# Keys of 42 chunks turned through device memory instead of on TensorE

## What is computed

```python
q = jax.nn.relu(q) + EPS                      # q, k, v = layernorm(x) @ Wq, Wk, Wv
k = jax.nn.relu(k) + EPS
k_cumsum = jnp.cumsum(k, axis=2)
context = jnp.cumsum(jnp.einsum('bhnd,bhne->bhnde', k, v), axis=2)
D_inv = 1.0 / jnp.einsum('bhnd,bhnd->bhn', k_cumsum, q)
attn = jnp.einsum('bhnd,bhnde,bhn->bhne', q, context, D_inv)
x = x + attn @ Wo + bo
...
gate, y = fp4_linear(x, w_gate), fp4_linear(x, w_up)
x = x + fp4_linear(jax.nn.silu(gate) * y, w_down)
```

## Time and profile before

| | |
|---|---|
| median of 3 runs | 1554.55 us (1552.29 to 1557.08) |
| the profiled execution | 1555.95 us, of which the span from first to last instruction is 1553.7 us |
| granted TensorE clock | 0.997 of full speed |
| PE busy | 1500.2 us, 97% |
| PEld, DVE, ACT, POOL busy | 90%, 73%, 41%, 47% |
| DMA packets on SP's queue | 159120, 129.75 MB, 28.2% of 16 engines' time |

### The profile page before, as it was taken

The page is one execution under the profiler, slowest core; times in us unless marked ns, Lnnn a source line. Parts: engine busy times, 40 slices in busy tenths (PEclk is TensorE's granted clock), DMA queues, the critical chain, the costliest instruction groups (busy, mean ns, idle before and its releaser), DMA issues.

```text
span 1553.7 us, 55070 instructions
## 1 busy us (share of the span) xinstructions
PE 1500.2 (97%) x23652; PEld 1400.9 (90%) x23652; DVE 1131.7 (73%) x2322; ACT 644.2 (41%) x1165; POOL 727.4 (47%) x822
## 2 busy tenths in 40 slices
PE   8989999999999999999999999999999999999998
PEld 7888899889989999999889989899999999989998
DVE  8787676867777777676767777767767777767767
ACT  6433344344443344444344443444443343442433
POOL 4322454443554444554443555444554544554543
PEclk9999999999999999999999999999999999999999
DMA  4102233233233223233233233233233232232210
GB/s 165 33 2 58 71 97 110 79 88 98 82 97 107 87 83 101 79 97 110 75 93 93 86 98 101 78 98 93 77 107 93 80 103 84 83 110 85 75 58 16
DMA packets 159360, 133.25 MB, mean 86 GB/s; under 512 B 12944, under 2 KB 150672, under 8 KB 159120
## 3 DMA queue, kind: packets, MB, share of 16 engines
q1 hardware_dynamic: 159120, 129.75, 28.2%
HBM read 68.09 MB, written 61.60 MB: 83 GB/s over the span
## 4 chain that ended last, share of the span: by engine, by line
issue 23%; PE 18%; DVE 17%; POOL 15%; DMA 13%; SPq 7%; ACT 3%; DVEq 0%; POOLq 0%; ACTq 0%
PE bank L591 12%; DMA attn<-attn_away 4%; DMA hq_away<-hq_blocks 4%; DMA attn_away<-probs 4%; POOL attnT_lo L1499 4%; DVE attn L1861 3%; DVE hq_blocks L1930 3%; SPq L530 3%; POOL hqT_lo L1511 3%; POOL x_bias L1460 2%; POOL xq L1538 2%; POOL hq L1487 2%; SPq L547 2%; ACT attnT_hi L1185 1%; PE bank L795 1%
## 5 line engine op out<-in xcount | busy, mean ns | idle before, releaser
L591 PE MATMUL bank<-xT_hi,wqk_hi 128*128 128x256 f32 x1024 | 211.3, 288 | 1.3 <-DVE hqT_lo L1679 1.3
L591 PE MATMUL bank<-xT_hi,wqk_lo 128*128 128x256 f32 x1024 | 203.7, 280 | 0.0
L591 PE MATMUL bank<-xT_lo,wqk_hi 128*128 128x256 f32 x1024 | 203.6, 280 | 0.0
L1538 POOL TENSOR_TENSOR xq<-x_scaled,x_scale 128x256 f32<-128x256 f32 x64 | 57.9, 904 | 310.6 <-DVE x_scaled L1726 310.6
L1112 ACT ACTIVATE qkT<-bank 128x512 f32<-128x512 f32 x256 | 148.5, 592 | 122.7 <-PE bank L591 120.4
L1499 POOL TENSOR_TENSOR attnT_lo<-attn,attnT_hi 128x1024 fp32r<-128x1024 f32 x58 | 156.9, 2705 | 62.3 <-ACT attnT_hi L1185 62.3
L1559 POOL TENSOR_SCALAR qkT<-qkT 128x512 f32<-128x512 f32 x256 | 158.4, 631 | 34.3 <-ACT qkT L1112 33.2
L591 PEld LDWEIGHTS bank<-xT_hi,wqk_hi 128*128 128x128 f32 x1024 | 157.2, 188 | 5.1 <-issue 1.9
L591 PEld LDWEIGHTS bank<-xT_hi,wqk_lo 128*128 128x128 f32 x1024 | 156.7, 188 | 0.0
L591 PEld LDWEIGHTS bank<-xT_lo,wqk_hi 128*128 128x128 f32 x1024 | 156.6, 188 | 0.0
L1235 ACT ACTIVATE silu<-bank 128x352 f32<-128x352 f32 x128 | 58.4, 457 | 229.2 <-PE bank L591 229.2
(11 more groups left out here) (219 smaller groups left out, 3869.9 us busy)
## 6 DMA issues: line engine op xcount, KB each, us to landing
attn<-attn_away SPq DMA_DIRECT2D x232, 128.0 KB, 2.9
hq_away<-hq_blocks SPq DMA_DIRECT2D x58, 384.0 KB, 3.2
hq<-hq_away SPq DMA_DIRECT2D x232, 96.0 KB, 2.2
attn_away<-probs SPq DMA_DIRECT2D x58, 256.0 KB, 2.7
attn_away<-probs SPq DMA_DIRECT2D x116, 128.0 KB, 2.7
x_in<-in_L_attn_x SPq DMA_DIRECT2D x32, 256.0 KB, 2.9
out<-out_sb SPq DMA_DIRECT2D x64, 128.0 KB, 2.6
qkT<-in_L_attn_Wq SPq DMA_DIRECT2D x1, 1024.0 KB, 7.5
```

The lines of the kernel that those rows point to most:

```text
L591: at = pe.matmul(dst, lhs_at(kt), rhs_at(kt), start=first and kt == 0, stop=last and kt == k_tiles - 1)
L1538: pool.tensor_tensor(blocks(xq[:], XB), blocks(x_scaled[:], XB), each(x_scale[:], XB), ALU.mult).then_inc(xq_ready, 1)
```

## The change

For 42 chunks (`SENT_K`: those from chunk 6 to 61 with c < 3) TensorE's 8 transposes and ACT's 2 copies are gone. Instead DVE transposes the 32x32 blocks of the keys straight from `qkT` into `probs` (`block_k`), SP sends `probs` to one of two buffers in device memory (`k_away`), and eight DMAs fetch it: four for the rows and heads that the early keys read, four for the late ones. The two parts lie in different halves of `k_tok`, so each waits only for the readers of its own half in the chunk before. Both chunks of a unit are blocked by DVE in the odd step ahead of the unit.

In `k_tok` the columns of a head come in the order in which pairs are grouped; `head_keys` finds them. The order in which query and key tiles are projected is changed, so that the four key tiles come first, and `scores` now waits for six tiles of the unit, not four, before its first product. The early keys are ahead of probs by values for every c. SP's order in odd steps is changed: `send_attn` now stands between `send_hq` and `fetch_hq`.

```diff
+    SENT_K = [g for g in range(WARM + 2, END) if g % CHUNKS < CHUNKS - 1]
...
+        k_away = nc.dram_tensor("k_away", (2, P, INNER), F32, kind="Internal").ap()
...
-        QK_ORDER = [0, 4, 2, 6, 1, 5, 3, 7]
+        QK_ORDER = [4, 5, 6, 7, 0, 2, 1, 3]
+        def first_pairs_ready(u):
+            return PAIRS * u + (6 if u else 4)
...
+        k_blocks = probs[:, 0:INNER].rearrange("p (a h c j) -> p h j a c", a=GROUPS, h=2, c=GROUP)
...
+            def send_k(n):
+                sp.wait_ge(k_blocks_ready, sent_k(n) + 1)
+                if sent_k(n) > 1:
+                    sp.wait_ge(early_k_back, 16 * GROUPS * (sent_k(n) - 1))
+                    sp.wait_ge(late_k_back, 16 * GROUPS * (sent_k(n) - 1))
+                sp.dma_start(k_away[sent_k(n) % 2], probs[:, 0:INNER]).then_inc(k_sent, 16)
+            def fetch_k(n, late, back):
+                at = k_away[sent_k(n) % 2].rearrange("(i r) (a h e) -> a h r i e", r=GROUP, a=GROUPS, h=2)
+                to = k_tok[:].rearrange("p (h i e) -> p h i e", h=2, i=GROUPS)
+                for a in range(GROUPS):
+                    h = int((a >= GROUPS // 2) != late)
+                    sp.dma_start(to[GROUP * a:GROUP * (a + 1), h], at[a, h]).then_inc(back, 16)
+            def fetch_early_k(n):                       # fetch_late_k: the same with kv_done
+                sp.wait_ge(k_sent, 16 * (sent_k(n) + 1))
+                sp.wait_ge(kv_early_done, (CHUNKS - 1) * b + c)
+                fetch_k(n, False, early_k_back)
...
                 if c % 2 == 0:                          # SP, after store(g - 4)
+                    if g in SENT_K:
+                        fetch_late_k(g)
+                    if g + 1 in SENT_K:
+                        fetch_early_k(g + 1)
...
                 else:
+                    if g in SENT_K:
+                        fetch_late_k(g)
                     if g - 3 in SENT_HQ:
                         send_hq(g - 3)
+                    if g in SENT_ATTN:
+                        send_attn(g)
+                    if g - 3 in SENT_HQ:
                         fetch_hq(g - 3)
                     if g in SENT_ATTN:
-                        send_attn(g)
                         fetch_attn(g)
+                    if g + 1 in SENT_K:
+                        send_k(g + 1)
+                        fetch_early_k(g + 1)
+                    if g + 2 in SENT_K:
+                        send_k(g + 2)
...
-                pe.wait_ge(qk_ready, PAIRS * u + 4)
+                pe.wait_ge(qk_ready, first_pairs_ready(u))
...
-                if c == 0:
-                    early_keys()
+                early_keys()
...
-                    if c and not first:
-                        early_keys()
...
-                    turn_k(b, c, g)
+                    if g not in SENT_K:
+                        turn_k(b, c, g)
...
+                if n == 0 and g in SENT_K and c % 2 == 0:      # DVE, mask
+                    dve.wait_ge(k_sent, 16 * sent_k(g + 2))
...
+            def block_k(n):
+                t = n % 2
+                dve.wait_ge(qk_ready, PAIRS * (n // 2) + 4)
+                dve.wait_ge(attn_sent, 48 * sent_attn(n - t))
+                if sent_k(n):
+                    dve.wait_ge(k_sent, 16 * sent_k(n))
+                dve.transpose(k_blocks, qkT[:, PAIRS:2 * PAIRS, t * P:(t + 1) * P].rearrange(
+                    "p (h j) (a c) -> p h j a c", h=2, c=GROUP)).then_inc(k_blocks_ready, 1)
...
                 gated_by_silu(g - 2, 0)                        # DVE, odd_step
+                if g + 1 in SENT_K:
+                    block_k(g + 1)
                 if exists(u + 2, ALL_HALVES):
                     ln1_begin(u + 2, c // 2)
...
                 begin_h(g - 2)
+                if g + 2 in SENT_K:
+                    block_k(g + 2)
```

More of the change, by code:

```diff
@@ L1318, in even_step @@
                     square_h(g - 3)
[L1319 to L1320 removed]
+                if g not in SENT_K:
+                    for n in range(2):
+                        keys_to_tokens(b, c, n)
                 high_xq(g - 2)
```

44 lines of the change are left out of this document (32 added, 12 removed).

## The result

The changed kernel takes 1586.51 us in the median of four runs (1582.08 to 1588.4), the kernel before 1553.42 beside it: a ratio of 1.0212 with a 95% interval of 1.0191 to 1.0233. It is slower by 33 us; 1538 was predicted, and the range ended at 1565.

A forecast was written before the change was run, and what follows sets the result against it. PE, busy 1500.2 of 1553.7 us, and its few waits were taken to set the end. Gains of 14 x (0 + 0.9 + 0.3) = 17 us gave 1538, with 8 in 10 runs from 1518 to 1565.

The forecast's parts named there:

- The rest: Remaining parts: fewer ACT copies, early keys ahead of probs, key tiles first, early and late fetches; taken as worth nothing.
- the block transpose: DVE's transpose of keys with a write step of 4 elements: taken as 1.22 us, bounds 1.2 and twice 1.22.
- slow transpose: Rival, chance 0.09: DVE's strided transpose takes twice as long, the second send lands at T + 4.8, 1567 us.
- The memset of the earlier trace: Nearest strided write on record: two of 32 columns, 65 apart, in 0.14 us, read as about a column a cycle.
- cost nothing: Even step, c = 0: DVE's block transposes lie in 4.17 us of its idle time, so themselves cost nothing there.
- set the copy: Even step, c = 0: with attn early, POOL's L1499 ends T + 2.3 (T: end of x's turn), mask possible at T + 2.5.
- c = 1, gain 0: Odd step: PE arrives 1.09 us earlier at the turn of xq and waits as much longer for DVE's second normalization.
- c = 2, attn early, gain 0.9: Even step: attn sent 4.2 us earlier, `project_v` starts T + 2.9 instead of T + 3.85; bounds 0.3 and 1.1.
- c = 0, gain 0.3: Even step: early attn helps, but the mask waits for the second send, T + 3.3 in the mean; bounds +1.1 and -1.7.
- The landing of a send: 512 KB of keys to device memory: taken as 3.6 us, from 384 KB in 3.2 and three DMAs in 3.8.
- PE's clock keeps its level: If the stall moves about 1.3 us to one place, PE's clock holds, as it does now with a 2.10 us stall.

The follow-up runs named there:

- ln1_first_no_sends: Against blocks_only, the first block transpose of keys in each odd step moved behind the next unit's layernorm statistics (ln1), still no sends or fetches of keys: 1518.34 us.
- step_of_2: The changed kernel with keys written and read at a step of 2, each send as four DMAs, first block transpose behind ln1; reference's values: 1598.86 us, 1.0265.
- no_keys: The changed kernel with keys' columns read side by side and without block transposes, sends and fetches of keys (old keys, same products): 1514.31 us, 0.9732.
- blocks_only: Against no_keys, DVE's block transposes of keys put back, written side by side, still no sends, fetches or waits for them: 1542.02 us, 0.9907.

## Why the prediction was wrong

**The step that failed is the price of the two stepped accesses.** One of them was not priced at all: the sum and "The rest" have no term for the state products, while the new layout in `k_tok` makes PE read its weights with a step of 4 elements. 3072 products went from 222 to 278 ns in the mean, and 15 to 18 us of time. The other, the block transpose, was taken as 1.22 us and measured 2.07, inside the bounds of 1.2 and 2.44; it cost 25 to 28 us, where the rival forecast 29 (1567 - 1538) for a transpose of 2.44. The rival "slow transpose", given 0.09, is the one whose mechanism came true. The memset of the earlier trace rows, for which 1.22 was kept, misled. Two of 32 columns in 0.14 us are 2.2 ns a column, not the transpose's 1.2, so the row did not say what was read from it. It shows no price for its step either: adjacent memsets of 256 and 520 columns take 0.27 and 0.49 us in the same trace, which gives, as an estimate, 0.08 us for 32 adjacent columns, and each of the two took 0.085. Why a memset has no price that a transpose has is open. The Trainium skill ("SBUF — State Buffer", Specifications (TRN2)) was right against the row: its sentence asks for at least two hits in each 16-byte line, which a step of 4 misses and a step of 2 just meets, and 2068 and 1246 ns fit that. But by another passage of that page of the Trainium skill (the note on cachelines under "Door 1: The DMA port swizzle (why `[64,N]` ≈ `[32,N]`)") four fp32 would be a free stride. The trace has 2068 ns for it: there the measurement decides.

**The block transposes "cost nothing", and POOL "set the copy" at T + 2.3: mis-sized.** With both accesses at the old price the kernel takes 1547 (0.9934), 10 us faster than before and not 17. That the two lie so near is partly luck: the early attn alone brings 33 us, where the sum had 17 for everything, and the turning of keys takes 22 of them back (0.9934 - 0.9789). The second transpose is hidden as predicted (ln1_first_no_sends). The first is not: it pushes ln1 by 2.3 us, 1.2 of work and 1.1 of waiting for the attn sends, where I had counted about 1. Without the step L1563 ends at T + 2.8 for c = 0, with it at T + 3.2.

**c = 1, gain 0: right in its place, with a smaller wait.** The turn of xq waits 9.1 us, over 15 steps, for the normalization; in before it was 3.4. That is 0.4 us more a step, where 1.1 was forecast; without any turning of keys it is 0.5, and the step is as long as with it.

**c = 2, attn early, gain 0.9: right as a mechanism, too small in size, and lost again.** Alone it moves `project_v` from T + 3.69 to 2.58, 1.1 us, and shortens the step by 1.26. In after POOL is late again, and `project_v` comes at T + 3.39.

**c = 0, gain 0.3: wrong in both directions.** Attn early alone shortens this step by 1.06, the upper bound of my 0.3; the keys' path then takes it back and more: 15.16 to 15.81. The mask was expected at T + 3.3 and starts at T + 4.2.

**The landing of a send, taken as 3.6 us: right.** The median of 42 is 3.6 (2.6 to 5.0). The serial chain (first landing, four fetches, second landing, mask) shows in the rows of step_of_2.

**"PE's clock keeps its level": not in every step.** In the middle of after, TensorE's granted clock falls behind the stall of three even steps with c = 2, as it does in two of before. It is a small part of the 33 us, but it makes the same stall dear in one step and cheap in the next.

**The sum, rebuilt from the ratios in us** (0.001 is 1.55): attn early -33; tile order and early keys +3, which is no difference; transposes off PE -12; block transposes at 1.2 us +27; sends and fetches +4; stepped write +25; stepped weights +18. That is +32, for the 33 measured. The steps from 1514 to 1547 depend on the order in which they are taken.

What is not settled: in after, 3 of 14 even steps with c = 2 last 18.5 to 18.6 us against a median of 16.2, at a lower clock behind the stall (below), and a fourth lasts 17.1 at full clock. Other kernels have between none (no_keys) and 14 (step_of_2) steps with such a fall, so the clock has a share in the differences above; no run takes it by itself. Nor was a staging buffer of its own for the keys' blocks tried.

## What to carry to other kernels

Price every reader of a tensor whose layout changes, not only the writer: the transposes left TensorE, and 43 of the 45.8 us of busy time came back in its own state products. When a part is meant to be hidden in an engine's idle time, ask what stands behind it on that engine and who waits for that: with no sends in the way, the same 52 us of work cost 27 us ahead of ln1 and 2 to 4 behind it. And try the parts of a change one by one, since the one that paid here was four lines of DMA order.

## What was not expected of the hardware

For these two instructions a step of 8 bytes in SBUF is free, and one of 16 or 32 bytes is not: 1246, 2068 and 2152 ns for the write of a 128x1024 fp32 block transpose on DVE (1242 side by side), 135, 213 and 214 ns for a 64x64 fp32 weight load on TensorE (135 side by side).

A DVE instruction with two tensor inputs of 128x704 takes 0.89 us with POOL idle and 2.01 with POOL's products and additions beside it (798.50 above, where POOL works without a break from 797.92). In after it is 0.89 in the 30 cases in which POOL is idle, and 2.02 in the median of the 29 in which POOL works all through. Its mean over the run went from 1034 to 1407 ns. The block transpose ahead of it pushed it into POOL's work: the mean is 997 in no_keys and 1417 in blocks_only, and 1358 in ln1_first_no_sends, where ln1 is not late:

```profile
L1783 DVE SCALAR_TENSOR_TENSOR h_scaled<-hid,h_inv 128x704 f32<-128x704 f32 x62 | 87.3, 1407 | 2.1
```

TensorE's clock fell behind some stalls and not behind others as long. In the even step at T = 750.37 PE was busy for 1.79 of 3.5 us, and in the next 3.5 us the granted clock was 0.55, near the lower of its two levels (1.2 and 2.4 GHz), with pairs of products at 1.06 us instead of 0.63; the windows view (stretch, length, busy us of PE, PEld, DVE, ACT, POOL, clock, DMA share, GB/s):

```profile
751.00:754.50 3.50, 1.79 (x84) 1.49 (x78) 3.43 (x4) 1.49 (x4) 2.63 (x2) 1.00 0.37 115
754.50:758.00 3.50, 3.47 (x9) 2.81 (x10) 3.11 (x5) 0.60 (x1) 0.28 (x2) 0.55 0.13 38
```
```profile
754.53 0.93 PE L651 MATMUL bank<-wv_hi,xT_hi 128*128 128x512 f32 x2 [1.74 <-DVE state L1916]
755.25 1.06 PE L651 MATMUL bank<-wv_lo,xT_hi 128*128 128x512 f32 x2
```

In the even step at T = 943.83 of the same trace PE waited 1.70 us at the same place, and the granted clock stayed at 1.00.
